# Sparse groups of a graph network layer in bursts of two instead of one

## The reference

```python
src_h = h[src] @ W_msg.T + b_msg
msg = src_h + edge_embed[clip(edge_type, 0, 8)]
messages = segment_sum(msg, dst, num_segments=12500)
r = sigmoid(i_r + h_r); z = sigmoid(i_z + h_z); n = tanh(i_n + r * h_n)
h_new = (1 - z) * n + z * h        # i_* from messages, h_* from h
x = layernorm(x + h_new)
```

## Time and profile before

| | us |
|---|---|
| median of 3 runs | 1082.27 (1081.86 to 1085.27) |
| span of the profiled execution (its own time, first to last instruction) | 1255.1 |
| PE busy | 1037.9 |
| DVE busy | 859.2 |
| POOL busy | 733.5 |
| ACT busy | 660.5 |

### The profile page before, as it was taken

The page is one execution under the profiler, slowest core; times in us unless marked ns, Lnnn a source line. Parts: engine busy times, 40 slices in busy tenths (PEclk is TensorE's granted clock), DMA queues, the critical chain, the costliest instruction groups (busy, mean ns, idle before and its releaser), DMA issues.

```text
span 1255.1 us, 23526 instructions
## 1 busy us (share of the span) xinstructions
PE 1037.9 (83%) x8411; PEld 656.5 (52%) x8411; DVE 859.2 (68%) x2699; ACT 660.5 (53%) x1283; POOL 733.5 (58%) x779
## 2 busy tenths in 40 slices
PE   5456677888888988989889989889888888888884
PEld 2124354555555555556556656555555555555552
DVE  8413557677776877868777767777876777676644
ACT  4243404455655555656666656555655556554622
POOL 7725645665566666666666666566666666566640
PEclk9566568999999999999999999999998999999996
DMA  8529311222222322322333223223323233332321
GB/s 244 159 79 310 107 33 53 78 77 74 74 77 79 91 77 77 91 78 77 82 83 92 79 78 92 74 79 92 90 77 89 76 89 83 86 92 80 83 81 28
DMA packets 94565, 114.23 MB, mean 91 GB/s; under 512 B 19820, under 2 KB 80616, under 8 KB 94441
## 3 DMA queue, kind: packets, MB, share of 16 engines
q0 software_dynamic: 35264, 73.19, 21.8%
q1 hardware_dynamic: 57320, 37.79, 10.2%
q10 hardware_dynamic: 1856, 1.66, 0.5%
HBM read 96.56 MB, written 16.00 MB: 90 GB/s over the span
## 4 chain that ended last, share of the span: by engine, by line
PE 64%; issue 10%; DVE 9%; ACT 7%; another core or an unknown queue 7%; DMA 1%; SPq 1%; DVEq 0%; ACTq 0%
PE psf L1097 28%; PE psb L1082 14%; PE pAB L1026 5%; PE psg L1065 4%; PE pAB L1040 4%; ACT mem L1213 3%; DVE ohl L868 2%; PE pAB L1043 2%; DVE ohk L862 2%; PE psg L1069 2%; PE psf L1102 1%; DMA arena<-in_x 1%; ACT mem L1153 1%; DVE ohk L865 1%
## 5 line engine op out<-in xcount | busy, mean ns | idle before, releaser
L604 POOL DMA_INDIRECT xg<-x_split,idx x648 | 616.1, 951 | 392.1 <-PE psg L1069 151.0
L1213 ACT CAST mem<-psb 128x432 f16<-128x432 f32 x896 | 426.7, 525 | 398.4 <-PE psb L1082 300.8
L1097 PE MATMUL psf<-mem 128*128 128x384 bf16 (+1 forms) x2744 | 618.4, 330 | 13.6 <-issue 6.8
L1082 PE MATMUL psb<-ohk,ohl 128*128 128x108 bf16 (+3 forms) x1865 | 421.6, 264 | 97.9 <-issue 57.4
L862 DVE TENSOR_TENSOR ohk<-table_bank,prm 128x392 bf16<-128x392 f16 (+3 forms) x437 | 271.0, 620 | 108.6 <-PE psb L1082 69.1
L1097 PEld LDWEIGHTS psf<-mem 128*128 128x128 f16 (+1 forms) x2744 | 240.4, 99 | 131.3 <-issue 34.9
L1082 PEld LDWEIGHTS psb<-ohk,ohl 128*128 128x128 bf16 x1865 | 173.6, 100 | 251.3 <-issue 116.4
L868 DVE TENSOR_TENSOR ohl<-table_bank,prm 128x512 bf16<-128x512 f16 x437 | 180.8, 414 | 0.0
L891 DVE TENSOR_TENSOR mem<-mem,psg 128x136 f32 (+9 forms) x184 | 54.9, 298 | 168.4 <-remote 106.8
L604 POOL DMA_INDIRECT xg<-in_x,idx x88 | 84.2, 957 | 76.3 <-PE psg L1069 44.7
L865 DVE TENSOR_TENSOR ohk<-table_bank,sort 128x40 bf16<-128x40 f16 (+3 forms) x437 | 106.5, 244 | 0.0
(11 more groups left out here) (148 smaller groups left out, 808.4 us busy)
## 6 DMA issues: line engine op xcount, KB each, us to landing
xg<-x_split,idx POOLq DMA_INDIRECT x648
x_split<-mem SPq DMA_DIRECT2D x24, 384.0 KB
xb<-in_xT SPq DMA_DIRECT2D x49, 128.0 KB
arena<-in_x SPq DMA_DIRECT2D x24, 256.0 KB
arena<-in_xN SPq DMA_DIRECT2D x47, 128.0 KB
out<-spill SPq DMA_DIRECT2D x19, 128.0 KB
out<-arena SPq DMA_DIRECT2D x144, 8.0 KB
out<-arena SPq DMA_DIRECT2D x15, 128.0 KB
```

Source lines behind the costliest of these rows:

```text
L604: pool.indirect_dma_start(out=xg[:, p % RING, :] if split else xg32(p % RING), out_offset=None, in_=x_d if split else x, in_offset=bass.In ...
L1082: ins = pe.matmul(psb[:, bank % NB, held * HC:(held + m) * HC], ohl[:, e % KB, :], ohk[:, e % KB, d * HC:(d + m) * HC], start=(k == 0), st ...
L1097: pe.matmul(psf[:, 0:3 * H], Bb[q % 2][0:kk, HT + h, :], xs[0:kk, h, :, :].rearrange("p c f -> p (c f)"), start=(h == 0), stop=(h == HI - ...
L1213: act.copy(Bb[q % 2][:, :, n:n + MOST], psb[:, bank % NB, 0:MOST * HC].rearrange("p (d h) -> p h d", h=HC)).then_inc(S["s_eb"], 1)
```

## The change

Two groups (`PAIR`) now form one burst. Items `("G", g)` exist for even g alone. The burst has 24 matmuls of x (8 in fp32 for the first 22 groups) and 8 of the types, with group g in the first and group g+1 in the second part of the same bank, and one signal that raises `s_used` by 8. DVE builds the one-hots of both in one pair of operations, into two buffers of double size (`AHEAD` = 2, the SBUF for it comes from `wihc`, which becomes the same memory as `wih`). Both additions, still one instruction for each group, stand half a group's chunks behind the burst (`ADD_AT`). The window width of both is that of the wider one. The condition of a gather is unchanged in form, but `s_used` now moves in steps of 8.

```diff
-AHEAD = 3
+AHEAD = 2
+ADD_AT = 0.5
...
-        chunks = [[("G", g)]]
+        first_of_pair = g % PAIR == 0
+        base = g - g % PAIR
+        chunks = [[("G", g)] if first_of_pair else []]
...
-        outs = [step(g, place(T0 * P + 512 * g)) for _ in range(n)]
+        outs = [step(base, place(T0 * P + 512 * base)) for _ in range(n)]
...
-        chunks[min(1, len(chunks) - 1)].append(("GA", g))
+        if first_of_pair:
+            chunks[round(ADD_AT * (len(chunks) - 1))] += [("GA", g + k) for k in range(PAIR)]
...
-WG = [width(g) for g in range(GROUPS)]
+WG = [max(width(g - g % PAIR + k) for k in range(PAIR)) for g in range(GROUPS)]
...
-        g2 = psg[:, 0:2 * W].rearrange("p (a w) -> p a w", a=2)
+        g2 = psg[:, 0:PAIR * 2 * W].rearrange("p (k a w) -> p k a w", k=PAIR, a=2)
...
-                        if g >= AHEAD:
-                            v.wait_ge(S["s_used"], G * (g - AHEAD + 1))
-                        v.tensor_tensor(onehots(g)[0], rel[:, g, :].unsqueeze(2).to_broadcast([P, G, w]),
+                        if g >= PAIR * AHEAD:
+                            v.wait_ge(S["s_used"], G * (g - PAIR * AHEAD + PAIR))
+                        v.tensor_tensor(onehots(g)[0],
+                                        rel[:, g:g + PAIR, :].rearrange("p g t -> p (g t)").unsqueeze(2).to_broadcast([P, n, w]),
...
-                        v.wait_ge(S["s_used"], G * (g + 1))
+                        v.wait_ge(S["s_used"], G * (g - g % PAIR + PAIR))
...
-                        v.tensor_tensor(d, d, g2[:, :, 0:WG[g]], ALU.add).then_inc(S["s_acc"], 1)
+                        v.tensor_tensor(d, d, g2[:, g % PAIR, :, 0:WG[g]], ALU.add).then_inc(S["s_acc"], 1)
...
-                            ahead.setdefault(("GA", own[a - back][1]) if a >= back else None, []).append(it)
+                            ahead.setdefault(("GA", own[a - back][1] + PAIR - 1) if a >= back else None, []).append(it)
...
-                        for j in range(G):
-                            p = g * G + j
+                        for j in range(PAIR * G):
+                            p, k = g * G + j, j // G
...
-                        ins.then_inc(S["s_used"], G)
+                        ins.then_inc(S["s_used"], PAIR * G)
```

More of the change, by code:

```diff
@@ L25 @@
 GROUPS = NG // G
+PAIR = 2
 EP = TILES * P
@@ L38 @@
 ND2 = 2 * NT
-TW = (G - 1) * ND2 + P
+TW = (PAIR * G - 1) * ND2 + P
 BIAS = (32, 64)
@@ L234, in schedule @@
     for g in range(GROUPS):
-        ub.append(float(clear - W))
-        top = place(min(E, T0 * P + 512 * (g + 1)))
-        assert top + MARGIN < clear - W
-        chunks = [[("G", g)]]
+        first_of_pair = g % PAIR == 0
+        base = g - g % PAIR
+        if first_of_pair:
+            ub += [float(clear - W)] * PAIR
+            top = place(min(E, T0 * P + 512 * (g + PAIR)))
+            assert top + MARGIN < clear - W
+        chunks = [[("G", g)] if first_of_pair else []]
         if g == 0:
@@ L247, in schedule @@
         n = STEPS[late is not None]
-        outs = [step(g, place(T0 * P + 512 * g)) for _ in range(n)]
-        lb.append(float(low))
+        outs = [step(base, place(T0 * P + 512 * base)) for _ in range(n)]
+        if first_of_pair:
+            lb += [float(low)] * PAIR
         while units and g >= LEAD and spent <= total * pace((g - LEAD) / (GROUPS - REST - LEAD)):
@@ L371, in gnn_kernel @@
         xg = sb("xg", [P, RING, 3 * H], BF16)
-        ohs = sb("ohs", [P, AHEAD, G * W])
+        ohs = sb("ohs", [P, AHEAD, PAIR * G * W])
         lbF = ohs[0:1, :, :].rearrange("p a w -> p (a w)")[:, 0:3 * GROUPS]
@@ L394, in gnn_kernel @@
         wih = sb("wih", [P, 3 * H])
-        wihc = sb("wihc", [P, 3 * H])
+        wihc = wih
         whh = sb("whh", [P, 3 * H])
@@ L1053, in _ @@
                         oh, oh16 = onehots(g)
[L1054 removed]
+                        pe.wait_ge(S["s_oh"], g // PAIR + 1)
                         if g:
                             pe.wait_ge(S["s_acc"], BEFORE[("GA", g - 1)] + 1)
[L1057 to L1058 removed]
+                        for j in range(PAIR * G):
+                            p, k = g * G + j, j // G
                             pe.wait_ge(s_g[p % RING], 16 * (p // RING + 1))
                             if g < SWITCH:
[L1061 to L1062 removed]
+                                ins = pe.matmul(g2[:, k, 0, 0:w], xg32(p % RING), oh[:, j, :], start=(j % G == 0),
+                                                stop=(j % G == G - 1), skip_group_check=True)
                             else:
                                 for c in range(3):
[L1065 to L1066 removed]
+                                    ins = pe.matmul(g2[:, k, 0, 0:w], xg[:, p % RING, c * H:(c + 1) * H], oh16[:, j, :],
+                                                    start=(j % G == 0 and c == 0), stop=(j % G == G - 1 and c == 2),
                                                     skip_group_check=True)
[L1068 to L1071 removed]
+                        for j in range(PAIR * G):
+                            ins = pe.matmul(g2[:, j // G, 1, 0:w], tohb[:, g // PAIR % AHEAD, j * ND2:j * ND2 + P],
+                                            oh16[:, j, :], start=False, stop=(j % G == G - 1), skip_group_check=True)
+                        ins.then_inc(S["s_used"], PAIR * G)
                     elif it[0] == "B":
```

25 lines of the change are left out of this document (9 added, 16 removed).

## The result

The changed kernel takes 1122.09 us (median of 4 runs, 1116.26 to 1126.67) against 1082.53 us (1081.86 to 1085.27) of the kernel before: 1.0348 times as long, 95% interval 1.0321 to 1.0375. The prediction said 1070, in a range of 1044 to 1089. The change costs 40 us instead of winning 12.

What follows compares the result with a forecast made beforehand. It took TensorE to bound the kernel, with only gaps to win. Terms of −19, −7, −3.3, −3 and +2 summed to −30 us in the profile, scaled by 0.4 to −12: 1082.3 to 1070 us, range 1044 to 1089.

Steps and rivals of the forecast that it cites:

- the signals: TensorE's gaps before dense slots: half of the slow burst signals go, 184 to 92; −19 us, bounds 0 and −32.
- the first groups: Early groups: one TensorE gap of 7.22 us behind a single group's signal goes; −7 us, bounds 0 and −15.
- the longer blocks on DVE: DVE: additions and pair operations take 1.61 us in a row against 0.95; +2 us, bounds 0 and +45.
- the later start of the final blocks: Final blocks start by the pair's first group, less than a period later, where they have slack: nothing.
- The end: Groups 180 and 181: one burst has no wait for an addition between them; −3.3 us, bounds 0 and −3.3.
- gathers not waited for by TensorE: Sign to look for in the profile after: TensorE has no waits for gathers; their coarser release costs nothing.
- One-hots on DVE: DVE: pair operations of 0.71 and 0.30 us, 27 us less work; −3 us from TensorE's waits for the reduction.
- Both additions later: DVE: additions half a group's units later let it prepare more slots before waiting; gain already counted, otherwise nothing.
- The rest: Wider windows under 1 us; same matmul count, `wihc` in place of `wih` and final blocks' start: nothing.
- signals at full price: Burst signals cost as much in timed runs as in the profile: −30 us, 1052; chance 0.17.
- The second: TensorE's gaps move, being due to ACT's and DVE's own work; only the end's gap goes: 1081; chance 0.15.
- The third: DVE's longer block starves TensorE in narrow stretches; 45 us at most in the profile, 1095 timed; chance 0.18.

Runs made afterwards that it cites:

- repeated profile: The kernel before, unchanged, profiled a second time: 1084.07 us timed, profiled span 1081.9 us.
- double burst alone: Changed kernel with TensorE's bursts and blocks by pairs, but DVE's additions and one-hots by single groups at their old places: 1096.64 us.
- late blocks alone: Kernel before, with the final blocks' start decided for both groups of a pair by the first of them: 1090.51 us.
- the unfit one: The first profile of the kernel before, which the prediction read: span 1255.1 us beside 1082.3 timed.
- the run with steps of 8: Kernel before, with each gather waiting until the pair of groups that holds its ring buffer is used: 1084.14 us.
- the fastest kernel: Kernel before with 16 dense one-hot buffers in place of 12 and a gather ring of 17 in place of 23: 1079.07 us.
- DVE's pair alone: Changed kernel with single-group bursts and signals; both additions and the pair's one-hots in one row behind the second burst, blocks by pairs: 1091.18 us.
- early pairs: Changed kernel with both additions and the pair's one-hots right behind the first unit after the burst: 1112.82 us.
- with sixteen buffers its wait: Changed kernel with additions behind the first unit after the burst, 16 dense one-hot buffers for 12, gather ring 17 for 23: 1108.37 us.
- the run at 0.25: Changed kernel with ADD_AT 0.25 in place of 0.5, additions a quarter of a group's chunks behind the burst: 1125.45 us.

## Why the prediction was wrong, step by step

Four steps of it failed: the signals, which it took 19 us off and which cost nothing; the first groups, from which it took 7 and which cost some 5; the longer blocks on DVE, for which it took 2 and which cost up to 16 and more by their place; and the later start of the final blocks, which it put at nothing and which costs 6.

**What it was read from.** The span stood 172.8 us over the timed median. The prediction saw that and scaled the sum by 0.4; it should have doubted the rows. It took 44 us for the gaps of a timed run, by letting its matmuls take 1037.9 us as in that profile, whose mean granted clock was 0.926. The repeated profile has a clock of 0.968, 989.4 us of matmuls and 92.5 us of gaps. That 92.5 of 217 is 0.43, beside the chosen factor of 0.4, is luck: the gaps were not where the sum had them. In the repeated profile the addition starts 0.14 us after a burst, and over the changed kernel's trace the release comes, in the median, 14 ns after the modelled end of the burst. There was no slow signal to save.

**Signals and first groups (−19, −7).** These two terms failed together: they sized gaps of one execution. TensorE's own waits for one-hots and for ACT in the repeated profile are 11.0 and 9.7 us, 20.7 together, where the term took 19 off 63.2 in the middle alone; from 260 to 1060 us they are 3.2 and 5.0. The 7.22 us behind an early group's burst are 0.60 there, at 85.65, and wait for a one-hot. Halving the signals won nothing that can be seen: the double burst alone costs 6 us more than its late blocks alone (1096.6 less 1090.5). By the Trainium skill ("TensorE: Matmul & The Clock Gate", The cost: per-tile semaphore tail), 92 fewer would be an estimate of 2.4 us; no run here shows even that, and none excludes it beside costs that are larger.

**The end (−3.3).** Read rightly, and won nothing. The gap stands in the repeated profile, and the changed kernel has none before a burst near there; but it has a longer one soon after, for a count that DVE makes, where the repeated profile has 0.65 us. First the repeated profile, then the changed kernel:

```profile
1049.51 0.68 PE L1065 MATMUL psg<-ohs,xg 128*128 128x88 bf16 x12 [3.31 <-issue]
1092.34 2.06 PE L1048 MATMUL pAB<-wih,mem 128*128 128x384 f32 x4 [3.88 <-DVE cnts L791]
```

From the end of the last burst to the end of the program it is 20.2 us in the one and 23.6 in the other.

**The first groups in fact cost time.** A double burst needs eight gathered tiles before any dense slot behind it can run. TensorE's timeline of the changed kernel's early groups, answering to the earlier trace rows:

```profile
76.13 2.37 PE L1069 MATMUL psg<-ohs,xg 128*128 128x52 f32 x10 [1.01 <-DVE tohb L854]
78.89 0.67 PE L1069 MATMUL psg<-ohs,xg 128*128 128x52 f32 x2 [0.39 <-DMA xg<-in_x,idx]
80.08 0.67 PE L1069 MATMUL psg<-ohs,xg 128*128 128x52 f32 x2 [0.52 <-DMA xg<-in_x,idx]
81.45 0.67 PE L1069 MATMUL psg<-ohs,xg 128*128 128x52 f32 x2 [0.70 <-DMA xg<-in_x,idx]
```

TensorE waits for gathers inside the burst. The first dense block's matmuls with x (L1097, now L1105) start at 103.7 us in the repeated profile, at 109.7 with the double burst alone and at 110.9 in the changed kernel. In the six profiles with single bursts (other than the unfit one) it is 103.6 to 106.6, in the ten with double bursts 108.9 to 110.9: some 5 us, in place of the 7 that were to be won. The step "gathers not waited for by TensorE" failed here; it held in the middle, and the run with steps of 8 shows the coarser release free.

**One-hots on DVE (0.71 and 0.30 us; 27 us less work).** The durations were right, the saving was not. The groups by line and shape of the changed kernel, answering to the earlier trace rows:

```profile
L851 DVE TENSOR_TENSOR ohs<-rel,table_bank 128x544 f32<-128x544 f16 x9 | 6.4, 713 | 0.0
L854 DVE TENSOR_TENSOR tohb<-typ,table_bank 128x144 bf16<-128x144 f16 x92 | 27.3, 297 | 0.0
```

Their durations sum to 94.7 us, 26.7 less than the 121.4 of the repeated profile, but DVE's busy time fell by 5.9 us only (855.4 to 849.5). Single operations overlap their neighbours slightly (605.22 and 605.36 above start before the one before them ends), and half as many operations overlap half as often, so most of the 26.7 had been done beside other work. And less work on DVE was worth nothing: the reduction, for which −3 us was taken, is waited for 9 us longer.

**Both additions later (nothing).** The prediction said that DVE would have more slots ready. It costs 9 us instead, against both additions early, and up to 13 at 0.25. Standing at a burst's signal was cheap: DVE stood there 55.2 us in the repeated profile and 56.0 in the fastest kernel's, the one with sixteen buffers, and every run that took this wait away by a later place was slower than the kernel before.

**Longer blocks (+2, bounds 0 to +45).** The term that was mis-sized: at the first unit behind a double burst the row costs 16 us (1112.8 against 1096.6 with single rows). Its working missed a piece. The row of four is 1.64 us from its first start to its last end, near the 1.61 forecast, but only because operations that don't wait for each other overlap a little (0.17 us here), which pays for most of the 0.21 us that the second addition stands for the first. In the repeated profile a single group's row, with that overlap and no such wait, is well under the forecast's 0.95: it starts at 604.63, and the next dense one-hot at 605.36, 0.73 us later. In the changed kernel that distance is 1.57 us (540.68 to 542.25), more than two single rows: pairing saved DVE nothing there. Moving the one-hots between them gave back 11, 9 and 7 us in three variants. The cost hangs on the place of the row. Behind the first unit of the second group it is next to nothing, with single bursts (DVE's pair alone, 7 us of which 6 are the blocks) and with double ones (1097.8 against 1096.6). In the first group's chunks the same row costs 12 to 28 us more than that, at four places (1109.7 to 1125.5 against 1097.8).

**The rest (nothing).** Final blocks started by the pair's first group cost 6 us alone, by a copy of ACT that comes behind a stage of theirs and that TensorE waits for. "Less than a period later, in the middle where they have slack" was not read from any row.

**The sum of what was shown.** Blocks 6, double burst 6, the second addition's wait 9 to 11, and 6 for the remaining meeting of both (1101.7 less 1084 less 12): 29 us for early pairs, and 9 for the place, together 38 of 40. This is one order of taking the parts away, by differences between medians that are each good to some 3 us; in another order they come out otherwise. At the second group's place the 6 for the meeting are gone, and with the one-hots between the additions there, the double burst's 6 are gone too (1090.7 against 1090.5 with late blocks alone).

TensorE's own time gives a second account, of the changed kernel against the repeated profile, 38.9 us: busy +9.6; waits for one-hots +13.5, for the reduction +8.8, for ACT's copies of closed blocks +5.6, for gathers +4.3, for the groups' own one-hots +2.9, at the end +3.2, before bursts −7.1 (7.8 to 0.7); the rest −1.9. So the late blocks, the start and DVE's longer rows are all in it. Whether the busy time is longer by the lower clock or because matmuls that follow a wait overlap less is not separated: bursts of one with later additions have 996.4 us of it at a clock of 0.970.

**The rivals.** The first, signals at full price, has no ground without slow signals. The second was right that TensorE stands for ACT's and DVE's own work, which is what the repeated profile names, but not that the time would stay. The third was nearest in mechanism (DVE's longer block, waits for one-hots up from 11.0 to 24.5 us) and gave 1095 with a chance of 0.18. That its bound, 45 us, is near the measured 40 is luck: half of it was DVE standing at the addition until a double burst is done, and the changed kernel's trace has 5 such waits. It isn't the whole either: with sixteen buffers its wait is nearly gone and the time moves by 4 us.

**Open.** Why additions at 0.25 and 0.5 make TensorE wait more than both early and late ones. Their neighbours in DVE's queue were the theory that fell with the run at 0.25. The table shows which of TensorE's waits grow, not why at these places. Whether the long row is as dear in the first group's chunks behind single bursts was not run.

## What to carry to other kernels

Compare the profiled span with the timed median before reading a single gap: where they differed by 16%, DVE's busy time still held (859.2 and 855.4 us), TensorE's was 5% too long (1037.9 and 989.4) and most of the waits were not the kernel's, and a second profile of the same kernel was worth more than any scaling. Ask of a queue that feeds the bound engine what stands at each place of it, and try the place before the grouping: the same operations at five places gave 1098 to 1125 us, a spread of 28 where the whole change was to win 12. Time in which the feeding engine waits for a signal that comes anyway was cheap here. Of two small operations where the second waits for the first, put other work between them. And a stage moved by less than a period can land before the one copy that the bound engine waits for.

## What the runs showed of the hardware

In one profiled execution of the kernel before, releases by TensorE's bursts came up to some 4 us after the end of the matmuls, 1.17 us in the median of 184, while in a repeat of the same program and in the changed kernel they came 14 ns after, in the median. By the Trainium skill ("Perfetto Trace Analysis", Tensor Engine Instruction) a matmul's end is computed by the profiler. That could shift ends, but the span itself was 173 us longer than the timed median, so time was really lost. What caused it stays open.

An addition that waits for the semaphore raised by the one right before it on DVE starts 0.21 us after that one ends (median of 92, 20.6 us in all), where operations that don't wait follow with no gap or overlap slightly (542.03 and 542.25 above, 0.07 us before the end of the one before). A raise of a semaphore by 8 for two groups showed no difference to a raise by 4: the median release is 14 ns after the burst's end in both, over 92 and 184 bursts.
